# Equivariant messages: products summed over edges by TensorE, a 128-row radial matmul, and VectorE's small steps moved

## The reference, cut to what matters

```
x = layernorm(x + attention layers(x))
R = relu(w_edge * w1 + b1) @ w2 + b2                # per edge: 1 -> 64 -> 384 radial weights
Y = spherical harmonics of the edge vector          # per edge: 1, 3 and 5 numbers
for each block of outputs (8 scalars; 8 vectors) and of inputs (8 scalars; 8 vectors):
    acc += norm * einsum("euv,ef,evi,ofi->euo", R_block, Y_block, x[src], W3J)
out.at[dst].add(msg)                                # msg: 32 numbers per edge
x = layernorm(x + out)
```

## Time and profile before

| what | value |
|---|---|
| median of three runs | 7120.96 us |
| profiled execution, its own time | 7123.42 us |
| its span, first to last instruction | 7121.3 us |
| mean granted TensorE clock | 0.804 |
| TensorE matmul busy | 5928.9 us (83%) |
| TensorE weight load busy | 4528.5 us (64%) |
| VectorE busy | 6159.4 us (86%) |
| ScalarE busy | 3368.9 us (47%) |
| GpSimd busy | 4853.9 us (68%) |

### The profile page before, as it was taken

One profiled execution on the slowest core, in us unless ns is written; L12 is line 12 of the kernel. 1 busy time (PEld: TensorE's weight loads), 2 busy tenths in 40 slices (PEclk: granted clock), 3 DMA queues, 4 the chain that ended last, 5 costly groups with the idle time before them and its releaser, 6 DMA issues.

```text
span 7121.3 us, 170234 instructions
## 1 busy us (share of the span) xinstructions
PE 5928.9 (83%) x26044; PEld 4528.5 (64%) x26045; DVE 6159.4 (86%) x12236; ACT 3368.9 (47%) x10977; POOL 4853.9 (68%) x7291
## 2 busy tenths in 40 slices
PE   0589898897579889898668898888866999999998
PEld 0366666665456666666446666666555888888887
DVE  7689999897679999999668999999868999999999
ACT  0155555555135555555414555555623444444444
POOL 1788888781388878886068788887325666666665
PEclk8899999999599999999879999999965555555555
DMA  2211111111011111112011111111101111111111
GB/s 86 61 35 35 36 35 39 35 36 11 13 38 36 39 33 36 36 36 32 0 27 41 34 35 36 35 40 34 18 1 46 32 31 31 32 31 31 32 31 29
DMA packets 214545, 237.87 MB, mean 33 GB/s; under 512 B 72925, under 2 KB 195902, under 8 KB 213950
## 3 DMA queue, kind: packets, MB, share of 16 engines
q1 hardware_dynamic: 93630, 163.53, 7.7%
q0 software_dynamic: 120704, 72.40, 7.4%
HBM read 222.44 MB, written 13.20 MB: 33 GB/s over the span
## 4 chain that ended last, share of the span: by engine, by line
PE 35%; DVE 25%; issue 20%; DVEq 13%; POOL 5%; DMA 1%; POOLq 1%; ACT 0%; ACTq 0%; SPq 0%
PE psum L672 15%; PE psum L657 11%; DVE xs L1557 4%; PE psum L659 3%; DVEq L1225 3%; DVEq L1542 3%; POOL xg L502 3%; DVE acc L1569 2%; DVE u L1191 2%; PE psum L645 2%; DVE acc L1232 2%; DVEq L1021 2%; DVE u L1551 1%; DVE oht L1186 1%; PE psum L648 1%
## 5 line engine op out<-in xcount | busy, mean ns | idle before, releaser
L502 POOL DMA_INDIRECT xg<-table,idx x2808 | 2883.7, 1027 | 714.2 <-PE psum L648 252.5
L657 PE MATMUL psum<-wz,xt 128*128 x5928 | 1822.6, 401 | 49.8 <-ACT xt L922 49.7
L672 PE MATMUL psum<-px,oh 128*128 128x272 f32 x5616 | 1645.1, 417 | 258.6 <-DVE acc L1232 242.9
L672 PEld LDWEIGHTS psum<-px,oh 128*128 128x128 f32 x5616 | 961.9, 191 | 653.2 <-DVE acc L1232 437.8
L657 PEld LDWEIGHTS psum<-wz,xt 128*128 128x128 f32 x5928 | 1001.8, 197 | 408.2 <-issue 65.6
L557 POOL DMA_INDIRECT xg<-table,idx x936 | 911.7, 974 | 507.2 <-DVE xs L1557 282.3
L1191 DVE SCALAR_TENSOR_TENSOR u<-psum,atts 128x512 f32<-128x512 f32 x1482 | 1013.4, 684 | 218.8 <-PE psum L659 218.1
L803 PE MATMUL psum<-w2e,xt 65*128 65x256 f32 x1872 | 1057.0, 668 | 138.8 <-DVE xs L1557 74.1
L1199 DVE TENSOR_REDUCE lr<-u 128x16 f32<-128x512 f32 x1482 | 1012.6, 685 | 107.4 <-DVE u L1191 58.8
L1218 DVE TENSOR_TENSOR px<-xs,pg 128x528 f32 (+1 forms) x1404 | 990.3, 706 | 80.0 <-PE psum L672 39.8
L851 ACT ACTIVATE dist<-iota_f,ndloc 128x128 f32<-128x128 f32 x2808 | 974.2, 394 | 95.9 <-PE psum L672 73.3
(11 more groups left out here) (271 smaller groups left out, 7715.0 us busy)
## 6 DMA issues: line engine op xcount, KB each, us to landing
dr<-dlocs SPq DMA_DIRECT2D x468, 192.0 KB
xg<-table,idx POOLq DMA_INDIRECT x3744
at<-w_rows SPq DMA_DIRECT2D x156, 192.0 KB, 3.2
fl<-flags SPq DMA_DIRECT2D x30, 576.2 KB
flags<-fl SPq DMA_DIRECT2D x10, 576.2 KB, 3.2
table<-xn SPq DMA_DIRECT2D x3, 784.0 KB, 3.6
xp<-keys SPq DMA_DIRECT2D x5, 385.0 KB, 4.4
u<-keys SPq DMA_DIRECT2D x5, 385.0 KB, 4.5
```

Source lines behind the costliest of these rows:

```text
L502: nc.gpsimd.indirect_dma_start(out=xg[:, s % S6, t, 96:128], out_offset=None, in_=table, in_offset=bass.IndirectOffsetOnAxis(ap=idx[:, s, ...
L657: pe.matmul(out_z, xt[:, r, e * P:(e + 1) * P], wz[:, bass.ds(l, 1), :].rearrange("p o z -> p (o z)"), start=True, stop=False)
L672: last = pe.matmul(agg_ps(r), oh[:, s % 3, e, :], px[:, s % 3, e, :], start=(e == 0), stop=(e == 1))
```

## The change

`radial` takes all 128 partitions of the hidden tile: its rows 64 to 127 are set to zero once, row 64 to one, and rows 64 to 127 of `w2e` to zero before the weights are put into rows 0 to 64. Both groups of columns become one matmul of 384 columns into bank 2r+e.

The reduction of `pb` (L1569) and its array `mv` go. `pb` gets six slots instead of two, and `sum_messages` multiplies `pb` itself with the one-hot matrix: for each e two matmuls of 24 x 8 columns (t = 0 to 7, then t = 8 to 15) that add into the same columns of PSUM, read in runs of 8 with a pitch of 16 and written in runs of 8 with a pitch of 9. The 32 columns of `msg` go to the ninth place of each group of nine. VectorE then reduces 32 x 9 numbers from PSUM into `rp` (`sum_inputs`) and adds `rp` to `acc1` (`add_messages`) in the next step. The second instruction of `messages` goes.

On VectorE the block number is read at the start of `products`, `add_messages` stands between the two products, `prepare`'s product after the batch's last `pb`, its sum (`scalar_product`) after that step's reduction of `pa`. The first pass of the loop is written out.

```diff
             for e in range(2):
-                rows = hid[0:65, r, e * P:(e + 1) * P]
-                pe.matmul(z_ps(r, 0, HC)[:, e, :], rows, w2e[:, 0:HC], start=True, stop=True)
-                last = pe.matmul(psum[:, 4 + r, e * P:(e + 1) * P], rows, w2e[:, HC:HC + P], start=True, stop=True)
+                rows = hid[:, r, e * P:(e + 1) * P]
+                last = pe.matmul(psum[:, 2 * r + e, 0:HC + P], rows, w2e[:], start=True, stop=True)
...
         def sums_ps(r):
             return psum[:, 6 + r, 0:9 * C].rearrange("p (g t) -> p g t", t=9)
...
             pe.wait_ge(msg_done, HELD + batch + 1)
+            pe.wait_ge(pb_done, HELD + k + 1)
             pe.wait_ge(ad_done, HELD + k - 1)
+            parts = sums_ps(r)
             for e in range(2):
-                last = pe.matmul(psum[:, 6 + r, 0:C], oh[:, r, e, :], msg[:, s // 3, 2 * (s % 3) + e, 0:C], start=(e == 0), stop=(e == 1))
+                prod = pb[:, s, e].rearrange("p i (u t) -> p (i u) t", t=16)
+                for h in range(2):
+                    pe.matmul(parts[:, 0:24, 0:8], oh[:, r, e, :], prod[:, :, 8 * h:8 * h + 8],
+                              start=(e == 0 and h == 0), stop=(e == 1 and h == 1))
+            for e in range(2):
+                last = pe.matmul(parts[:, :, 8], oh[:, r, e, :], msg[:, s // 3, 2 * (s % 3) + e, 0:C], start=(e == 0), stop=(e == 1))
...
+            seq(op.memset(w2e[64:128, :], 0.0))
+            seq(op.memset(hid[64:128, :, :], 0.0))
+            for r in range(2):
+                op.memset(psum[:, 6 + r, 0:9 * C], 0.0)
...
         def products(k, s, batch, adds=None, summed=None, following=None):
+            b = block_of(summed) if summed is not None else None
             # waits, then pa = radial weights x features
+            if summed is not None:
+                add_messages(summed, b)
             # waits, then pb[:, s] = radial weights x vectors
-            b = block_of(adds) if adds is not None else None
+            if following is not None:
+                prepare(*following)
             # reduction of pa into msg
-            op.tensor_reduce(mv[:, half, n:n + 2, :], pb[:, r]..., AX.X, ALU.add).then_inc(vr_done, 1)
+            if following is not None:
+                scalar_product(*following)
             if adds is not None:
-                add_messages(adds, (s + 3) % S6, b)
+                sum_inputs(adds, (s + 3) % S6)
...
         def messages(k, half, batch):
+            # msg[:, half, :, 0:24] = along x unit vector, directly
-            op.tensor_tensor(msg[:, half, :, 0:24], rp, mv[:, half], ALU.add).then_inc(msg_done, 1)
...
+        def sum_inputs(k, s):
+            v.wait_ge(ag1_done, AHEAD + k + 1)
+            v.wait_ge(ad_done, HELD + k)
+            op.tensor_reduce(rp, sums_ps(s % 2), AX.X, ALU.add).then_inc(rp_done, 1)
+
+        def add_messages(k, b):
+            v.wait_ge(rp_done, HELD + k + 1)
+            sums = acc1[:, bass.ds(b, 1), :].rearrange("p o c -> p (o c)")
+            op.tensor_tensor(sums, sums, rp, ALU.add).then_inc(ad_done, 1)
```

More of the change, by code:

```diff
@@ L176, in z_ps, with sums_ps @@
             return psum[:, 2 * r:2 * r + 2, lo:hi]
+        def sums_ps(r):
+            return psum[:, 6 + r, 0:9 * C].rearrange("p (g t) -> p g t", t=9)
         def xt_ps(r):
@@ L253, in gatv2_program @@
         wb = at[0:64].rearrange("p a b -> p (a b)").rearrange("p (s e) -> p s e", s=S6)
-        mv = in_l1([2, 6, 24])
-        rp = in_l1([6, 24])
+        rp = in_l1([C])
         tq = in_l1([3, 6, 24])
@@ L261, in gatv2_program @@
         hid = xt
-        w2e = sb("w2e", [65, 384])
-        pb = xs[:].rearrange("p a b c d -> p (a b c d)")[:, 0:4 * 384].rearrange("p (a e i x) -> p a e i x", a=2, e=2, i=3)
+        w2e = sb("w2e", [P, 384])
+        pb = xs[:].rearrange("p a b c d -> p (a b c d)")[:, 0:S6 * 768].rearrange("p (a e i x) -> p a e i x", a=S6, e=2, i=3)
         w2raw = xs[:].rearrange("p a b c d -> p (a b c d)")[0:65, 2048:2048 + 384]
@@ L348, in gatv2_program @@
         pb_done = sem("pb_done")
-        vr_done = sem("vr_done")
         dm_done = sem("dm_done")
@@ L1505, in _ @@
             raw11 = w2raw[:, 192:384].rearrange("q (u v k) -> q u v k", v=8, k=3)
-            wa = w2e[:, 0:256].rearrange("q (u t) -> q u t", t=16)
-            wbd = w2e[:, 256:384].rearrange("q (u t) -> q u t", t=16)
+            seq(op.memset(w2e[64:128, :], 0.0))
+            wa = w2e[0:65, 0:256].rearrange("q (u t) -> q u t", t=16)
+            wbd = w2e[0:65, 256:384].rearrange("q (u t) -> q u t", t=16)
             op.tensor_scalar(wa[:, 0:8, 8:16], raw[:, 0], n0 * y0, None, ALU.mult)
@@ L1521, in _ @@
             seq(None)
-            for counter in (pa_done, pr_done, pb_done, vr_done, dm_done, dt_done, t_done, q_done, rp_done, msg_done, ad_done):
+            for counter in (pa_done, pr_done, pb_done, dm_done, dt_done, t_done, q_done, rp_done, msg_done, ad_done):
                 v.sem_inc(counter, HELD)
@@ L1529, in prepare, with scalar_product, products @@
                     v.wait_ge(gat[s], 32 * LAYERS * NBODIES + 32 * i + 32)
-                rows = feat[:, 3 * half:3 * half + 3].rearrange("p s e f -> p (s e) f")
-                f5 = rows[:, :, 16:56].rearrange("p n (i v) -> p n i v", i=5)
+                f5 = feat[:, 3 * half:3 * half + 3].rearrange("p s e f -> p (s e) f")[:, :, 16:56].rearrange("p n (i v) -> p n i v", i=5)
                 unit5 = unit[:, bass.ds(i * S6 + 3 * half, 3)].rearrange("p s e i -> p (s e) i")
-                r5 = lambda a: unit5[:, :, a:a + 3].unsqueeze(3).to_broadcast([P, 6, 3, 8])
-                t0 = tq[:, 0].rearrange("p n (i v) -> p n i v", i=3)
                 v.wait_ge(dt_done, HELD + batch)
-                op.tensor_tensor(t0, f5[:, :, 0:3], r5(0), ALU.mult).then_inc(dm_done, 1)
+                op.tensor_tensor(tq[:, 0].rearrange("p n (i v) -> p n i v", i=3), f5[:, :, 0:3],
+                                 unit5[:, :, 0:3].unsqueeze(3).to_broadcast([P, 6, 3, 8]), ALU.mult).then_inc(dm_done, 1)
+            def scalar_product(i, half, batch):
                 v.wait_ge(pa_done, HELD + i * S6 + 3 * half - 3)
                 v.wait_ge(dm_done, HELD + batch + 1)
-                op.tensor_reduce(rows[:, :, 0:8], t0.rearrange("p n i v -> p n v i"), AX.X, ALU.add).then_inc(dt_done, 1)
+                op.tensor_reduce(feat[:, 3 * half:3 * half + 3].rearrange("p s e f -> p (s e) f")[:, :, 0:8],
+                                 tq[:, 0].rearrange("p n (i v) -> p n v i", i=3), AX.X, ALU.add).then_inc(dt_done, 1)
             def block_of(k):
                 return v.value_load(brow[0:1, bass.ds(k, 1)], min_val=0, max_val=BLOCKS - 1)
-            def products(k, s, batch, adds=None):
+            def products(k, s, batch, adds=None, summed=None, following=None):
                 r, half, n = s % 2, s // 3, 2 * (s % 3)
+                b = block_of(summed) if summed is not None else None
                 v.wait_ge(rr_done, AHEAD + k + 1)
@@ L1570, in products @@
                 if adds is not None:
-                    add_messages(adds, (s + 3) % S6, b)
+                    sum_inputs(adds, (s + 3) % S6)
             def messages(k, half, batch):
                 v.wait_ge(pr_done, HELD + k + 3)
-                v.wait_ge(msg_done, HELD + batch)
-                along = rp.rearrange("p n (i u) -> p n i u", u=8)
-                op.tensor_tensor(along, msg[:, half, :, 32:40].unsqueeze(2).to_broadcast([P, 6, 3, 8]),
+                op.tensor_tensor(msg[:, half, :, 0:24].rearrange("p n (i u) -> p n i u", u=8),
+                                 msg[:, half, :, 32:40].unsqueeze(2).to_broadcast([P, 6, 3, 8]),
@@ L1579, in messages @@
                                  unit[:, bass.ds(k, 3)].rearrange("p s e i -> p (s e) i")[:, :, 0:3].unsqueeze(3).to_broadcast([P, 6, 3, 8]),
-                                 ALU.mult).then_inc(rp_done, 1)
-                v.wait_ge(rp_done, HELD + batch + 1)
-                v.wait_ge(vr_done, HELD + k + 3)
-                op.tensor_tensor(msg[:, half, :, 0:24], rp, mv[:, half], ALU.add).then_inc(msg_done, 1)
-            def add_messages(k, s, b):
+                                 ALU.mult).then_inc(msg_done, 1)
@@ L1587, in add_messages @@
+            def sum_inputs(k, s):
                 v.wait_ge(ag1_done, AHEAD + k + 1)
                 v.wait_ge(ad_done, HELD + k)
+                op.tensor_reduce(rp, sums_ps(s % 2), AX.X, ALU.add).then_inc(rp_done, 1)
+            def add_messages(k, b):
+                v.wait_ge(rp_done, HELD + k + 1)
                 sums = acc1[:, bass.ds(b, 1), :].rearrange("p o c -> p (o c)")
-                op.tensor_tensor(sums, sums, psum[:, 6 + s % 2, 0:C], ALU.add).then_inc(ad_done, 1)
+                op.tensor_tensor(sums, sums, rp, ALU.add).then_inc(ad_done, 1)
@@ new lines, in two_batches @@
+            def two_batches(i, starts):
+                k = i * S6
+                for s in range(3):
```

(20 more changed lines are left out.)

6 lines of the change are left out of this document (3 added, 3 removed).

## The result

The changed kernel takes 7013.2 us (7010.3 to 7017.4, 4 runs) where the kernel before takes 7121.6 us (four runs with it): a ratio of 0.9849, 95% interval 0.9837 to 0.9861, 108 us faster. The forecast was 6996 us. The profiled execution took 7017.4 us with a span of 7015.3. On two other chips the kernel before itself took 7914 and 7824 us, and the experiments that ran there are set beside those times.

The account below looks back on a forecast made before the run. VectorE (10.55 us a batch) was taken as the bound, TensorE and GpSimd close; GpSimd's 10.08 next. 154 x (10.885 - 10.08) = 124 us, with +1.7 and -3.2, gives 125.5: 7120.96 to 6996 us; range 6972 to 7110, own range 6985 to 7030.

Parts of the forecast that it names:

- GpSimd sets the pace at 10.08 us a batch: Equivariant part: GpSimd's unchanged work becomes the largest; batch goes from 10.885 to 10.08 us, 154 times, 124 us gained.
- VectorE 10.55 with some waits, TensorE 10.3 close behind: Kernel before, equivariant part: order of limits per batch, VectorE 10.55, TensorE 10.3, GpSimd 10.08 us, within 8%.
- Set-up: Ahead of the start signal: new memsets with the two drains cost +1.7 us.
- Tail: From the last gather's start T to the last addition: T + 20.9 instead of T + 24.1, -3.2 us.
- VectorE's prices: VectorE's steps: new 288-number reduction 0.37 us, small instructions 0.22 each; 8.9 to 9.3 us a batch, about 80% busy.
- `prepare`'s wait: VectorE's earlier `prepare` waits for the batch's three gathers: about zero, taken only from the later wait for `cross`.
- TensorE's price: TensorE's radial, products and `msg` columns at 2.4 GHz: 3.06 to 3.22 us a step, 9.2 to 9.7 a batch.
- The clock: TensorE, equivariant part: with all 128 rows filled instead of 65, 2.4 GHz from the second or third step on.
- Rival 1: VectorE and TensorE taking turns eat half the gain: 10.5 us a batch, gain 59 us, 7060 us; 18%.
- Rival 2: TensorE's clock stays at 1.2 GHz: 18.4 us a batch, + 1155 us, about 8275 us; 7%.
- Rival 3: Product matmuls' PSUM writes with gaps take twice the time: 13.4 us a batch, + 387 us, 7508 us; 11%.
- Rivals 4 and 5: 4: pace set elsewhere, nothing gained, 7121 us, 4%. 5: GpSimd gets faster too, 9.9 us a batch, 6970 us, 2%.

## Why the prediction was right, step by step

The measured 7013 us lie 17 us above the forecast and inside its own range of 6985 to 7030.

*GpSimd sets the pace at 10.08 us a batch*: right. The mean from batch 2 to batch 155 is (6965.11 - 5407.71) / 153 = 10.18 us, against 10.885, and the two runs with one gather show the bound arriving on GpSimd with the change. My 124 us from this term is 108. My reading of the pace that it left was incomplete: *VectorE 10.55 with some waits, TensorE 10.3 close behind* was VectorE alone, with a longer batch at each turn of the loop. The sum took the measured 10.885, so this cost nothing in it; it is why I expected 50 us of the 128-row radial alone, which gave 9. The 0.10 us a batch that I missed has two sources in the trace. Eight batches of 10.4 to 11.8 us, five of them with a wait of 2.0 us before a gather (put down to "issue" three times), make 9 us; long batches occur at the same numbers (36, 53, 88, 105, 140) in the trace of before. And `cross` is slower beside VectorE. GpSimd's second product in the kernel before, then the groups of the changed kernel (mean ns before the second bar):

```profile
L576 POOL TENSOR_TENSOR acc<-xg,acc 128x144 f32<-128x144 f32 x156 | 68.9, 442 | 0.0
```

```profile
L1591 DVE TENSOR_TENSOR acc<-acc 128x144 f32<-128x144 f32 x156 | 97.2, 623 | 0.0
...
L577 POOL TENSOR_TENSOR acc<-xg,acc 128x144 f32<-128x144 f32 x156 | 80.2, 514 | 0.0
L581 POOL TENSOR_TENSOR acc<-acc 128x144 f32<-128x144 f32 x156 | 79.9, 512 | 36.5 <-POOL acc L577 36.3 <-DVE xs L1573 0.2
```

VectorE's L1591 (`messages`) takes 0.62 us where others of its size take 0.30, and in the timeline above its 6203.24 coincides with GpSimd's product at 6203.25. In the tail, where GpSimd has ended, it takes 0.30. GpSimd's product that starts with it is not slower (449 ns against 450 before), the next one is (514 against 442). With the old order GpSimd's mean batch is 10.13 us instead of 10.18.

*Set-up*: +1.5 us against my +1.7 (the first gather starts at 5387.52 instead of 5385.97). *Tail*: I forecast -3.2 us, it is nothing: the last addition comes 24.3 us after the last gather, before the change 24.1. This term was wrong by 3.4 us, the pace's by 16.

```profile
6981.82 0.95 DVE L1573 TENSOR_TENSOR xs<-psum,acc 128x768 f32<-128x768 f32 x1
...
6989.41 0.30 DVE L1591 TENSOR_TENSOR acc<-acc 128x144 f32<-128x144 f32 x1
...
6997.68 0.19 DVE L1606 TENSOR_TENSOR acc<-acc 128x32 f32 x1 [0.30 <-DVE acc L1600]
```

The last batch's first `pb` starts at T + 8.4, where I had T + 5.9, and `messages` at T + 16.0, where I had T + 14.4. From `messages` to the last addition are 8.3 us, where I had 6.5. The first of the three sums is the dear one, on TensorE:

```profile
6989.81 2.57 PE L818 MATMUL psum<-xs,oh 128*128 128x192 f32 x8 [1.96 <-DVE acc L1591]
6992.17 0.90 PE L821 MATMUL psum<-acc,oh 128*128 128x32 f32 x4
6992.89 1.88 PE L818 MATMUL psum<-xs,oh 128*128 128x192 f32 x8
```

TensorE stood for 1.96 us, and the sum behind it takes 3.08 us against my 1.8, at a granted clock of 0.56 from 6989.8 to 6992.8. The sum by what was measured: 106.2 us earlier at the last gather, nothing more after it, 106 of span. The terms do not cancel each other's errors: the pace brought less than forecast, and so did the tail.

*VectorE's prices*: the reduction of 288 numbers has a distance of 0.37 us, as forecast, and the small steps 0.22. Its busy time is 88% (441.3 of 500 us), not about 80%. *`prepare`'s wait* for the gathers is near zero (18 us in all over 156 batches, 11 of them at the first), as forecast.

*TensorE's price*: 3.03 us a step against 3.06 to 3.22. *The clock*: the level rose within the first 25 us and stayed up to the tail. My reason, that 65 rows hold it low, is confirmed for the kernel before by the 128-row radial alone. For the change it is not needed: radial can fill 65 rows and the clock is 0.99, so something else that came with the change carries it, most likely the 128-row products, though no run shows them without the wider radial matmul.

*Rival 1* (hand-overs): not the pace, but by my reading of the run with one gather they are the next thing under it, at 9.77. *Rival 2* (low clock): wrong, even with 65 rows. *Rival 3* (gaps in PSUM): wrong; its price of a factor of two appears only when the reading side has gaps too. The run that writes each column 36 bytes from the last shows 0.163 us, as for runs of 8; and the products' 1536 columns take 1.30 us where radial's 1536, written in plain runs, take 1.37. The Trainium skill ("PSUM — Partial Sum Buffer", Specifications (TRN2)) has any non-contiguous pattern slow matmuls significantly; here, for fp32 matmuls, the measurement differs and decides. Reads 64 bytes apart take 0.32 us and runs of 32 bytes 0.163 us. The Trainium skill ("SBUF — State Buffer", Specifications (TRN2)) has accesses pay that go to a new 16-byte line each time; the trace agrees.

*Rivals 4 and 5*: neither; GpSimd did not become faster but slightly slower.

## What to carry to other kernels

Before costing an edit on the busiest engine, work out the free-running period of every engine from the distances of its starts, over a whole turn of the loop; the difference to the nearest of them is what the edit can bring, here 10.885 - 10.08 of an engine that looked a third idle. Then look at that engine for small work that can go elsewhere: moving a copy of six integers and a register read brought 139 us on top of the change's 108, where both were measured beside a before of 7121 to 7125 us. When a matmul's operand is laid out, keep neighbouring numbers together on the side that is read (runs of 8 cost nothing here; single numbers, read and written with gaps, a factor of two). And run the kernel on more than one chip: here 1.5% on one was 0.3% on another, in a run with the same matmul times.

## What the runs showed of the hardware that was not expected

- An fp32 MATMUL instruction of 192 columns starts every 0.163 us whether it writes runs of 8 at a pitch of 9 or single columns 36 bytes apart; with the same single columns and its moving operand read in single numbers 64 bytes apart it is 0.32 us.
- Giving the radial matmul 128 rows instead of 65, with zeros in the added ones, took the granted clock from 0.50 to a mean of 0.85 while TensorE's busy time fell from 477 to 337 of 500 us. With the product matmuls of 128 rows in between, 65 rows in radial kept 0.99.
- A VectorE product of 144 columns that reads and writes SBUF takes 0.62 instead of 0.30 us when it starts with GpSimd's products, and the second of GpSimd's takes 0.51 instead of 0.44. VectorE's product that reads PSUM takes 0.69 us beside GpSimd's work (6204.29 above) as without it.
